# Two cross attentions: head sums in one pass in full precision, and a tail that keeps its tokens on rows

## The chip, the cores and the metric

The kernel runs on one core of a Trainium2 chip. The metric is device time in microseconds of one execution; lower is better. A core has TensorE (PE in the profile, with its weight loads as PEld), VectorE (DVE), ScalarE (ACT), GpSimd (POOL), SyncE (SP), whose only work here is to issue transfers, and 16 DMA engines.

## The reference, cut to what matters

Two decoder layers on x (8 batches of 100 tokens, 256 features), with a context of 8 x 361 rows of 256 features. All data is float32.

```python
x = x + tanh(g_xattn[0]) * xattn0(layernorm(x), ctx)    # 16 heads of 64
x = x + tanh(g_ffn[0])   * ffn0(layernorm(x))           # latent attention, 8 experts + shared one, dense
x = x + tanh(g_xattn[1]) * xattn1(layernorm(x), ctx)    # 16 heads of 16, masked, biases on q, k, v and o
x = x + tanh(g_ffn[1])   * ffn1(layernorm(x))           # 2 of 8 experts for each token, taken by distance
```

xattn0 is not attention over all keys. Each query row i of the 100 meets the keys i, i+100, i+200 and i+300 only (361 keys, the missing ones of the last group are padded), and the softmax runs over these four. ffn1 works like this:

```python
d2 = sum(xs*xs) + sum(centroid*centroid) - 2*xs@centroid.T     # xs is the layer norm of x
dist = sqrt(maximum(d2, 1e-12)); w, sel = top_k(dist, 2); w = softmax(w)
out = sum over the two experts of w * ((silu(xs@Wg+bg) * (xs@W1+b1)) @ W2 + b2)
```

## The kernel before

Features stand on the 128 partitions (two tiles of 128) and the 800 tokens along the free dimension; a `half` is 400 of them. Five engine programs are written out by hand, each a fixed sequence; they meet on semaphores. A product whose operands are split in a rounded high part and a low rest is taken in three one-pass products (fp32r); a product on float32 operands takes four passes and shows as two records of PE.

Stages, with their times in the profiled execution: norm and query of the first cross attention (to 41.5 us), its batch loop (to 223), its output product (to 241), ffn0's attention (to 353), ffn0's experts (to 450), the second cross attention's query and first keys (to about 485), its loop over 32 quads (to 623), its output product, norm and the routing (to 667.8), the 20 blocks of ffn1's experts (to the end).

**First cross attention, batch loop.** For batch b TensorE runs `keys(b)`, eight tiles of six one-pass products each (`project_a`), into PSUM banks 0 and 1, then `values(b-1)`, eight tiles of six products and one that spreads the softmax weights (`SPREAD`, `SES`). VectorE multiplies each key tile by the queries (`products`, L1707) into three `PROD` buffers, and between those runs the seven steps of the previous batch's softmax (L1715 to L1739, on 16 partitions, one for each head). ScalarE rounds each product tile to `PRODH` (L1145), GpSimd takes the rest `PRODL` (L1485), and `sim` sums the features of a head: two one-pass products with 16 output rows for each tile, over all eight tiles into one bank, three tiles behind the keys. Then `weigh` (L1751, L1754) multiplies and sums eight value tiles.

**Second cross attention, quad loop.** Quad q = 4b + g holds four heads of batch b. In iteration q TensorE takes `turned_scores(q)`, the `scores` of quad q+2 whose maxima VectorE finds (`top`, L2049), turns the maxima (L879), and runs `mix_v(q-1)`: 12 products of up to 122 x 32 by 100 columns into bank 6, four of them side by side in groups of 32 output rows. A head gives 16 rows of values and 16 rows of sums (the values buffer holds ones beside each head). When a batch's four quads are in, VectorE's `outs(b)`, in iteration 4b+5, shuffles the sums and copies the mixed rows (L2067, L2069), ScalarE inverts the sums by Ln and Exp, GpSimd divides and adds the value bias into `OT1` (L1565, L1568) and then builds the query slots of a later batch (`mask_queries`). `mix_v(4b+4)` waits for `outs(b)` because it writes the same bank.

**Tail.** Behind the loop TensorE multiplies `OT1` (four groups) by `WO1`: 16 products of 400 columns, half of them behind the last batch's division. ScalarE gates, VectorE adds to X, `norm(5)` follows, normed rows and X are transposed to tokens on rows (`rows_of`: `ROWS`, `RESID`), ScalarE squares them, and 16 small products give the dot products with the centroids. `route()` on VectorE picks two experts for each token, counts, and places each token in blocks of 128. Meanwhile VectorE has split the first expert's weights (`gu_low(0,0)`, `gu_low(0,1)`) right after the loop.

**SP's queue at that place** (order of issue): loads of expert weights 1 and 2, the bias rows, two down tables, a wait for `expert_weights_low_ready` N0+2 (both halves of `gu_low(0,*)`), the load of expert weights 3 into the buffer that these halves have read, a wait for `rows_copied`, the store of `ROWS` to DRAM, the store of `RESID` to the output. GpSimd gathers the first block's rows from DRAM when the first store has landed and `XROW` is known; the first expert product follows.

Of the kernel before, what the change touches and what calls it, by code (L numbers as in the profile page):

```python
# [7 lines left out]
F32 = mybir.dt.float32  # L8
# [15 lines left out]
P = 128  # L24
# [28 lines left out]
def program(nc, t):  # L53

    with ExitStack() as ctx:
# [24 lines left out]
        HS = sb("HS", [P, TI0 * H0])  # L80
# [8 lines left out]
        SM0 = sb("SM0", [H0, 6, S])  # L89
# [12 lines left out]
        def cut(region, at, n, parts=P):  # L102
# [6 lines left out]
        PROD = cut(RW, 8192, 1200).rearrange("p (s c) -> p s c", s=3)  # L109
        VSB = cut(RW, 9392, 1200).rearrange("p (s c) -> p s c", s=3)  # L110
        PV = cut(RW, 10592, 800).rearrange("p (s c) -> p s c", s=2)
        SE = cut(RW, 11392, 1200, H0).rearrange("p (s c) -> p s c", s=3)
# [13 lines left out]
        PRODH = part("PRODH", [P, 4, HALF], "XC", 0)  # L126
        PRODL = part("PRODL", [P, 4, HALF], "Y", 0)
        HSR = part("HSR", [P, TI0 * H0], "RB", 3328 + 4 * HALF)
# [41 lines left out]
        WO1 = cut(RW, 8464, 1024).rearrange("p (g c) -> p g c", g=4)  # L170
# [3 lines left out]

        KTHL = part("KTHL", [P, 2, KD, 2, KVE], "RW", 4032)
# [7 lines left out]
        OT1 = part("OT1", [P, 4, T], "XC", 0, F32)  # L183
        PTC = WK[:, :, :].rearrange("p s c -> p (s c)")[0:CH].rearrange("p (s c q) -> p s c q", s=2, c=3)
        SUMS, UN = STD[:, 0, :], STD[:, 1, :]
# [8 lines left out]
        CSQ = CENTS[0:S, 48:56]  # L194

# [6 lines left out]
        SQUARES = part("SQUARES", [S, B, D], "RO", B * D, F32)  # L202
        POSITION = part("POSITION", [S, 2 * B, P], "RO", B * D)
        RESID = part("RESID", [S, B, D], "RQ", GU1, F32)
# [55 lines left out]
            a_probs_low_ready a_products_high_ready a_products_low_ready a_keys_summed  # L260
# [9 lines left out]
            router_scores_shifted router_function_taken router_high_ready router_weights_spread  # L270
            router_spread_copied router_spread_copied_odd router_squares_ready gate_summed
# [3 lines left out]
            c_pads_set c_keys_summed c_keys_copied c_keys_low_ready c_query_low_ready  # L275
            c_values_summed c_values_copied c_scores_summed c_maximum_found c_maxima_low_ready
            c_maxima_turned c_maxima_placed c_turned_scores_summed c_exp_taken c_heads_mixed
            c_sums_inverted c_mixed_copied c_mixed_biased c_output_summed c_output_gated
            c_added_to_x mask_ready mask_stored c_query_turned_up c_query_stacked_even
            c_query_stacked_odd context_loaded3 c_query_slots_ready c_query_weights_scaled  # L280
# [14 lines left out]
        NORM = [(X, XC, "layer"), (X, Y, "layer"), (Y, XC, 0), (Y, XC, 2), (X, XC, "layer"), (X, XC, "layer")]  # L295
        LAYER = {0: 0, 1: 1, 4: 2, 5: 3}
# [25 lines left out]

        W_PIECES = [9, 11, 13, 15]

        LAG0 = 3

        def key_bank(b, m):

# [159 lines left out]
        def _(pe):  # L488
# [54 lines left out]
            def keys(b):  # L543
                pe.wait_ge(sem["a_context_low_ready"], b + 1)
                for ti in range(TI0):
# [6 lines left out]
                    if ti >= LAG0:  # L552
                        sim(b, ti - LAG0)
# [1834 lines left out]
```

## Time and profile before

| | us |
|---|---|
| median of three runs (lowest, highest) | 837.34 (836.78, 839.22) |
| the profiled execution | 836.42 |
| its span | 834.2 |
| PE busy | 745.0 (89%) |
| DVE busy | 562.8 (67%) |
| ACT busy | 414.6 (50%) |
| POOL busy | 241.5 (29%) |

The span runs from the first instruction to the last; the execution's own time is 2.2 us longer. Busy time is an average over stages with different limits: in the first cross attention VectorE is busy nearly all the time, in the quad loop TensorE works between short waits, and between 623 and 668 us the engines work one after another. PE records overlap each other, so their sum is more than the time the array streams.

### The profile page before, as it was taken

Reading aid. Unit: us, or ns where it says so; the run is one execution under the profiler, and the core shown is the slowest. Engines: PE = TensorE matmul, PEld = TensorE weight load, DVE = VectorE, ACT = ScalarE, POOL = GpSimd, SP = SyncE. Lnnn points to the kernel's source line nnn. Section 1 sums busy time; section 2 is a strip of 40 time slices with the busy share of each in tenths; the row PEclk is TensorE's granted clock in tenths of the full one; section 3 lists DMA queues with packets and bytes.
Section 4 is the critical chain, followed back from the end, with each engine's and each line's share of the span. In section 5 each row is a group of like instructions: output and inputs, shape, how many; then the busy total and the mean of one; then the engine's idle time right before and its main releaser. Section 6 shows DMA issues by size and latency. Waiting matters only on the chain.

```text
span 834.2 us, 13705 instructions
## 1 busy us (share of the span) xinstructions
PE 745.0 (89%) x4761; PEld 621.0 (74%) x4761; DVE 562.8 (67%) x1030; ACT 414.6 (50%) x896; POOL 241.5 (29%) x195
## 2 busy tenths in 40 slices
PE   6999999999889469989998898888998699999996
PEld 3588888889865168657996566666774699999995
DVE  3369999999728979737666567676554666656652
ACT  4544444443253249835434356565664545655651
POOL 0064544444003514510003302222212133433422
PEclk9999999999999979897999899998789599999999
DMA  6400000000070000000000766545052248999972
GB/s 235 200 2 18 19 19 19 19 1 1 1 279 9 0 0 3 1 1 1 1 9 1 182 158 150 132 108 172 2 195 95 86 163 291 328 304 309 328 227 57
DMA packets 29050, 86.01 MB, mean 103 GB/s; under 512 B 3759, under 2 KB 19599, under 8 KB 25655
## 3 DMA queue, kind: packets, MB, share of 16 engines
q1 hardware_dynamic: 25143, 79.89, 29.1%
q0 software_dynamic: 3840, 5.25, 3.0%
q8 instruction: 40, 0.66, 0.3%
q14 instruction: 27, 0.22, 0.1%
HBM read 74.75 MB, written 10.38 MB: 102 GB/s over the span
## 4 chain that ended last, share of the span: by engine, by line
PE 55%; DVE 14%; issue 4%; ACT 3%; DMA 2%; POOL 1%; POOLq 0%; SPq 0%; DVEq 0%; ACTq 0%
PE PS L490 51%; PE PS L1033 1%; DVE SM L2049 1%; DVE WK L1811 1%; DVE RW L1751 1%; PE PS L662 1%; DVE WK L1808 1%; DMA KST<-mask_rows 1%; DVE RO L1754 1%; PE PS L879 1%; PE PS L1003 1%; ACT SQ L1078 1%; POOL OT L1565 0%; DVE M L2058 0%; DMA out<-YO,TROW 0%
## 5 line engine op out<-in xcount | busy, mean ns | idle before, releaser
L1485 POOL TENSOR_TENSOR PRODL<-RW,PRODH 128x361 fp32r<-128x361 f32 x64 | 64.8, 1016 | 114.7 <-ACT PRODH L1145 111.1
L2049 DVE TENSOR_REDUCE SM<-PS 100x1 f32<-100x362 f32 x128 | 64.9, 531 | 46.5 <-PE PS L490 45.7
L490 PE MATMUL PS<-CTXH,WKV0H 128*128 128x362 f32 x256 | 85.8, 335 | 9.5 <-DVE RW L1707 8.9
L490 PE MATMUL PS<-CTXL,WKV0H 128*128 128x362 f32 x256 | 84.1, 328 | 0.0
L490 PE MATMUL PS<-CTXH,WKV0L 128*128 128x362 f32 x256 | 83.9, 328 | 0.0
L1334 ACT ACTIVATE WK<-PS 120x400 f32<-120x400 f32 (+1 forms) x96 | 48.3, 507 | 43.1 <-PE PS L490 42.2
L490 PEld LDWEIGHTS PS<-CTXH,WKV0H 128*128 128x128 f32 x256 | 48.3, 188 | 15.9 <-DVE RW L1707 11.0
L490 PE MATMUL PS<-KST,QST 97*100 97x362 f32 x128 | 54.4, 437 | 5.9 <-DMA KST<-mask_rows 3.3
L1592 POOL DMA_INDIRECT out<-YO,TROW x20 | 31.5, 1573 | 95.2 <-PE PS L1003 45.6
L1145 ACT CAST PRODH<-RW 128x361 fp32r<-128x361 f32 x64 | 31.8, 496 | 53.7 <-DVE RW L1707 53.4
L1754 DVE TENSOR_REDUCE RO<-RW 128x100 f32<-128x400 f32 x64 | 56.1, 877 | 2.2
L490 PE MATMUL PS<-RB,HTT 114*128 114x256 f32 (+1 forms) x240 | 55.2, 379 | 0.6 <-ACT HTT L1433 0.6
L2073 DVE TENSOR_TENSOR GUL<-RB,GUH 128x1368 fp32r<-128x1368 f32 x28 | 44.1, 1579 | 14.3 <-ACT GUH L1372 14.3
L1137 ACT COPY RW<-PS 128x361 f32<-128x361 f32 x64 | 29.5, 462 | 47.8 <-PE PS L490 46.4
L490 PE MATMUL PS<-GUH,XTH 128*128 128x342 f32 x160 | 51.6, 322 | 0.0
L490 PE MATMUL PS<-GUL,XTH 128*128 128x342 f32 x160 | 51.5, 322 | 0.0
L490 PE MATMUL PS<-GUH,XTL 128*128 128x342 f32 x160 | 51.3, 321 | 0.0
L490 PEld LDWEIGHTS PS<-RB,HTT 114*128 114x128 f32 (+1 forms) x240 | 44.7, 189 | 6.2 <-ACT HTT L1433 0.9
L490 PEld LDWEIGHTS PS<-CTXL,WKV0H 128*128 128x128 f32 x256 | 48.6, 190 | 0.0
L490 PEld LDWEIGHTS PS<-CTXH,WKV0L 128*128 128x128 f32 x256 | 48.2, 188 | 0.0
L1565 POOL TENSOR_TENSOR OT<-STD 128x400 f32<-128x400 f32 x8 | 11.2, 1395 | 120.7 <-ACT STD L1349 120.7
L1707 DVE TENSOR_TENSOR RW<-PS,RQ 128x400 f32<-128x400 f32 x64 | 36.2, 567 | 8.4 <-PE PS L490 7.5
(310 smaller groups left out, 1980.8 us busy)
## 6 DMA issues: line engine op xcount, KB each, us to landing
RB<-W SPq DMA_DIRECT2D x14, 1368.0 KB, 6.0
RB<-W SPq DMA_DIRECT2D x20, 768.0 KB, 7.1
KST<-keys_by_head SPq DMA_DIRECT2D x24, 362.0 KB
RQ<-W SPq DMA_DIRECT2D x6, 1368.0 KB, 6.1
keys_by_head<-KTHL SPq DMA_DIRECT2D x8, 724.0 KB, 3.3
CTX<-ctxT SPq DMA_DIRECT2D x16, 361.0 KB, 6.6
RW<-WGU SPq DMA_DIRECT2D x1, 2304.0 KB, 8.5
RW<-WKV SPq DMA_DIRECT2D x1, 2048.0 KB, 9.9
```

The lines of the kernel that those rows point to most:

```text
L490: return pe.matmul(out, lhsT, rhs, start=start, stop=stop)
L662: m = pe.transpose(PS[0:S, 4 + q, x * S:(x + 1) * S], PB[:, i % 3, (4 * q + x) * S:(4 * q + x + 1) * S], IDN[0:S, 0:S])
L1137: act.copy(VSB[:, i % 3, 0:KV], PS[:, 4 + i % 2, 0:KV]).then_inc(sem["a_values_copied"], 1)
L1145: act.copy(PRODH[:, i % 4, 0:KV], PROD[:, i % 3, 0:KV]).then_inc(sem["a_products_high_ready"], 1)
L1334: act.activation(PTC[0:CHT[c], q % 2, c, :], PS[0:CHT[c], 2 + c, 0:4 * S], ACT.Exp).then_inc(sem["c_exp_taken"], 1)
L1485: pool.tensor_tensor(low, raw, high, ALU.subtract).then_inc(sem["a_products_low_ready"], 1)
L1565: pool.tensor_tensor(o, UN.rearrange("p (g c) -> p g c", g=4), SUMS.rearrange("p (g c) -> p g c", g=4), ALU.mult).then_inc(sem["c_mixed_bi ...
L1592: pool.indirect_dma_start(t["out"], bass.IndirectOffsetOnAxis(ap=TROW[:, k:k + 1], axis=0), YO[:, k % 2, :], None, compute_op=ALU.add).the ...
L1707: dve.tensor_tensor(out, k, q, ALU.mult).then_inc(sem["a_products_ready"], 1)
L1754: dve.tensor_reduce(OT0[:, ti, tok(b)], PV[:, i % 2, :].rearrange("p (c i) -> p i c", c=NC), AX_X, ALU.add).then_inc(sem["a_heads_mixed"], 1)
L2049: dve.tensor_reduce(SM1[:, q % 2, j:j + 1], PS[0:S, i % 2, 0:KVE], AX_X, ALU.max, negate=True).then_inc(sem["c_maximum_found"], 1)
L2073: dve.tensor_tensor(GUL[k % 2][:, :, j, :], raw_gu(k, j), GUH[k % 2][:, :, j, :], ALU.subtract).then_inc(sem["expert_weights_low_ready"], 1)
```

## The change

1. First cross attention. `PROD` is kept in float32 in two buffers of four tiles, and `PRODH`, `PRODL` and their work on ScalarE and GpSimd are gone. `sim(b, quad)` takes four tiles at once: four float32 products of 128 x 32 by 361 columns, one to each group of 32 output rows. `sim(b, 0)` stands behind key tile 5, `sim(b, 1)` behind value tile 1 of the batch before. The softmax runs on 128 partitions instead of 16.
2. Second cross attention. `mix_v` reads the values buffer 16 columns earlier for odd quads, so that two quads fill 128 rows; `outs` has two parts of two instructions and a shuffle, each on 200 columns, and `divide` moves to VectorE. The value bias and `WO1` times the centroids are folded once (`fold_output`, `fold_centroids`), dot products of X with the centroids are taken in the loop (`dot_residual`), and X is turned to rows there (`turn_residual`).
3. Output: `project_out(b)` gives tokens on rows for one batch, 8 columns of centroid products and 256 of output in one accumulation of two products of 264 columns. VectorE adds these to the turned X, takes `bn_stats` and `bn_aggr`, and the norm is applied by ScalarE, one instruction for each batch.
4. Order: `gu_low(0,0)` moves into the loop (q = 29), `gu_low(0,1)` behind `route()`.

The diff, cut (semaphore renames and layout lines left out):

```diff
-    for b in range(B): ... (GpSimd: divide, add bias, mask_queries(b + 3))
+    for b in range(3, B):
+        mask_queries(b)
...
     def sim(b, quad):
+        pe.wait_ge(sem["a_products_ready"], 4 * i + 4)
+        for j in range(4):
+            m = mm(PS[32 * j:32 * j + 32, 2 + b % 2, 0:KV], HS[:, 32 * quad:32 * quad + 32],
+                   PROD[i % 2][:, j, 0:KV], quad == 0, quad == 1)
...
+    if (b, g) == (4, 0): fold_output()        # 8 small products, in mix_v
+    if (b, g) == (5, 0): fold_centroids()     # 4
+    if b == 6: dot_residual(g)                # 4 for each g
...
+    def project_out(b):
+        pe.wait_ge(sem["c_mixed_divided"], b + 1)
+        ...
+            pe.wait_ge(sem["c_rows_summed"], b - 2)
+        for c in range(2):
+            m = mm(PS[0:S, (0, 1, 7)[b % 3], 0:8 + D], OT1[:, c, tok(b)], WO1[:, c, :], c == 0, c == 1)
...
+    if q == QUADS: project_out(4)             # ahead of the last mix_v
+    if q in (24, 28, 29, 30): turn_residual(...)
+    if q in (30, 31): project_out(2 * q - 60); project_out(2 * q - 59)
...
     def outs(b):
+        link(dve.tensor_scalar(pair(OPPOSITE), mixed[:, :, 0, :], UPPER, None, ALU.mult))
+        link(dve.scalar_tensor_tensor(pair(OPPOSITE), mixed[:, :, 1, :], LOWER, pair(OPPOSITE), ...))
+        dve.stream_shuffle(SUMS, OPPOSITE, [q ^ 16 for q in range(32)])
+        link(dve.tensor_scalar(pair(UN), mixed[:, :, 0, :], LOWER, None, ALU.mult))
+        dve.scalar_tensor_tensor(pair(UN), mixed[:, :, 1, :], UPPER, pair(UN), ...)
...
+    for b in (5, 6, 7):
+        add_rows_in(b)
+        statistics(b)
     (ScalarE)
+    act.activation(RSTD, MOMENTS[:, :, 1], ACT.Ln, ...); act.activation(RSTD, RSTD, ACT.Exp, scale=-0.5)
+    act.preload_act_table_set("sqrt_and_others")
+    for b in range(B):
+        act.activation(ROWS[:, b, :], RESID[:, b, :], ACT.Identity, bias=SHIFTS[:, b:b + 1],
+                       scale=RSTD[:, b:b + 1]).then_inc(sem["rows_copied"], 1)
...
     route()
+    gu_low(0, 1)
     (SP)
     sp.wait_ge(sem["expert_weights_low_ready"], N0 + 2)
     load_weights(3)
-    sp.wait_ge(sem["rows_copied"], 4)
+    sp.wait_ge(sem["rows_copied"], B)
     sp.dma_start(XROWS..., ROWS)
```

## Rows read from the trace of the kernel before

**Rows 1.** Windows: span, length, busy us of PE, PEld, DVE, ACT, POOL, clock, DMA.
```profile
53.50:206.30 152.80, 144.35 (x851) 132.94 (x851) 145.98 (x224) 66.76 (x133) 73.16 (x64) 1.00 0.05 13
...
482.00:574.40 92.40, 82.79 (x823) 62.90 (x821) 62.89 (x150) 57.78 (x135) 19.60 (x16) 0.98 0.53 133
574.40:623.00 48.60, 42.71 (x463) 34.44 (x463) 26.29 (x70) 31.21 (x70) 8.65 (x8) 0.75 0.33 111
623.00:667.80 44.80, 35.00 (x160) 25.04 (x160) 26.64 (x65) 21.69 (x41) 8.39 (x6) 0.80 0.32 109
```

**Rows 2.** Timeline, first cross attention: start, length, engine, line, names, count, idle before.
```profile
53.51 0.57 DVE L1707 TENSOR_TENSOR RW<-PS,RQ 128x400 f32<-128x400 f32 x1 [3.15 <-PE PS L490]
...
119.83 0.56 DVE L1707 TENSOR_TENSOR RW<-PS,RQ 128x400 f32<-128x400 f32 x1
...
131.12 0.33 PE L490 MATMUL PS<-SES,SPREAD 128*128 128x362 f32 x1
...
132.63 0.33 PE L490 MATMUL PS<-SES,SPREAD 128*128 128x362 f32 x1
...
141.47 0.57 DVE L1707 TENSOR_TENSOR RW<-PS,RQ 128x400 f32<-128x400 f32 x1
```

**Rows 3.** Lines of the softmax: ns minimum/median/maximum, first and last start.
```profile
L1730 DVE TENSOR_TENSOR RW<-RW,SM x8: 561/807/810, 58.9 to 209.8; 16x400 f32<-16x400 f32 x8
...
L1736 DVE CAST SES<-RW x8: 356/653/668, 60.1 to 210.3; 16x400 fp32r<-16x400 f32 x8
...
L1739 DVE TENSOR_TENSOR SES<-RW,SES x8: 565/904/912, 61.3 to 210.7; 16x400 fp32r<-16x400 f32 x8
```

**Rows 4.** Timeline, one mix_v of the quad loop and the load behind it.
```profile
607.24 0.50 PEld L490 LDWEIGHTS PS<-WK,RQ 122*32 122x32 f32 x24 [0.17 <-issue]
...
607.90 0.16 PEld L490 LDWEIGHTS PS<-KST,QST 97*100 97x100 f32 x1 [0.15 <-issue]
```

**Rows 5.** Timeline, outs of one batch.
```profile
543.89 0.60 DVE L2067 STREAM_SHUFFLE STD<-PS 128x400 f32<-128x400 f32 x1
544.38 0.56 DVE L2069 COPY STD<-PS 128x400 f32<-128x400 f32 x1
```

**Rows 6.** Lines by form, quad loop: count, busy us, mean ns, idle before.
```profile
L2012 DVE SCALAR_TENSOR_TENSOR KTHL<-PS,COLS,KTHL 128x361 fp32r<-128x361 f32 x13 | 7.6, 586 | 3.5 <-ACT KTHL L1308 3.5
```

**Rows 7.** Waits of PE from 482 to 623 us: total us, times, longest.
```profile
PE PS L490 <- ACT WK L1334: 6.3, 4, 1.6
PE PS L490 <- DVE STD L2069: 4.8, 3, 1.6
PE PS L879 <- DVE M L2059: 1.6, 4, 0.4
```

**Rows 8.** Timeline, from the last mix_v to the first expert product.
```profile
620.78 2.23 PE L490 MATMUL PS<-WK,RQ 122*32 122x100 f32 x48
...
629.87 5.64 PE L490 MATMUL PS<-OT,RW 128*128 128x400 f32 x16 [0.92 <-POOL OT L1568]
...
646.75 0.32 SPq L470 DMA_DIRECT2D token_rows<-ROWS  x1
...
649.60 0.19 DVE L2124 TENSOR_SCALAR RT<-RT 100x64 f32<-100x64 f32 x1
...
652.80 0.16 DVE L2141 TENSOR_TENSOR RTC<-RT 100x8 f32<-100x8 f32 x1
...
662.12 0.48 DVE L2189 TENSOR_TENSOR WEIGHED<-RB,RT 100x320 fp32r<-100x320 f32 x1
662.39 1.30 POOL L1584 DMA_INDIRECT XB<-token_rows,XROW  x1 [25.29 <-DVE TROW L2186]
...
667.81 0.62 PE L490 MATMUL PS<-BROWS,PICKB 128*128 128x342 f32 x1 [1.02 <-issue]
```

**Rows 9.** Window of the small centroid products: PE records, clock.
```profile
645.30:646.90 1.60, 1.60 (x21) 1.00 0.00 0
```

**Rows 10.** Transfers from 621 to 660 us: count, KB each, us from issue to landing.
```profile
RB<-W SPq DMA_DIRECT2D x1, 1368.0 KB, 5.7
```

More of the change, by code:

```diff
@@ L439, in _ @@
             load(CENT, t["centT"], "moe1_small_loaded")
+            sp.wait_ge(sem["norm_variance_summed"], 10)
+            load(WO1T, t["WO1T"], "moe1_small_loaded")
             for b in range(B - 3):
@@ L589, in _ @@
                 else:
-                    for ti in range(TI0 - LAG0, TI0):
-                        sim(0, ti)
+                    sim(0, 1)
             project_out_a(0, 0)
@@ L911, in _ @@
                 ahead = q + 2 < QUADS
+                if q == QUADS:
+                    project_out(4)
                 if 0 <= q < QUADS:
@@ new lines, in outs @@
+                if b == 6:
+                    dve.tensor_copy(DOTS, PS[0:S, 6, 400:464].rearrange("p (b e) -> p b e", b=B))
+                dve.scalar_tensor_tensor(pair(UN), mixed[:, :, 1, :], UPPER, pair(UN), ALU.mult,
+                                         ALU.add).then_inc(sem["c_mixed_copied"], 1)
+                if b == 4:
+                    dve.tensor_tensor(CENT2, CENT2, ASIDE[:, 0:8].unsqueeze(1).to_broadcast([P, KD, 8]),
+                                      ALU.subtract).then_inc(sem["router_operand_ready"], 1)
@@ L2071, in gu_low, with statistics @@
+            def statistics(b):
+                dve.wait_ge(sem["c_rows_summed"], b + 1)
+                link(dve.bn_stats(PARTS6[:, b, :], RESID[:, b, :]))
+                dve.bn_aggr(MOMENTS[:, b, :], PARTS6[:, b, :]).then_inc(sem["c_statistics_found"], 1)
             def gu_low(k, j):
@@ L2081, in _ @@
                     top(q + 2, 1)
+                if g == 0 and b >= 2:
+                    divide(b - 2)
                 if g == 1 and b >= 1:
                     outs(b - 1)
+                if q == 29:
+                    dve.wait_ge(sem["c_values_summed"], 2 * B)
+                    gu_low(0, 0)
                 if g in (1, 2) and 0 <= b and b + 3 < B:
@@ L2091, in _ @@
                     keys_lo(2, q + 2)
-                if q == 24:
-                    dve.wait_ge(sem["moe1_small_loaded"], 32)
+                if q == 26:
+                    dve.wait_ge(sem["moe1_small_loaded"], 48)
                     dve.tensor_copy(PICKB[:, 0:E1], PICKED).then_inc(sem["router_result_ready"], 1)
+                    dve.wait_ge(sem["c_turned_scores_summed"], 12 * 6)
+                    dve.tensor_copy(TRI[:, :], TRIANGLE)
                 if q == -2:
                     stack_odd(1)
-            outs(B - 1)
-            dve.wait_ge(sem["router_scores_summed"], 2)
-            link(dve.tensor_copy(CSQ, PS[0:S, 7, 0:8]))
-            dve.tensor_copy(TRI[:, :], TRIANGLE)
-            gu_low(0, 0)
-            gu_low(0, 1)
-            add_to_x("c_output_gated", "c_added_to_x")
-            norm(5)
-            for i in range(4):
-                dve.wait_ge(sem["moe_turned"], 2 + i + 1)
-                dve.tensor_copy(ROWS[:, 2 * i:2 * i + 2, :],
-                                PS[0:S, i, :].rearrange("p (x c) -> p x c", x=2)).then_inc(sem["rows_copied"], 1)
+            for b in (0, 1):
+                add_rows_in(b)
+            for b in (0, 1):
+                statistics(b)
+            divide(B - 2)
+            for b in (2, 3):
+                add_rows_in(b)
+                statistics(b)
+            outs(B - 1)
+            add_rows_in(4)
+            statistics(4)
+            divide(B - 1)
+            for b in (5, 6, 7):
+                add_rows_in(b)
+                statistics(b)
             def route():
```

399 lines of the change are left out of this document (212 added, 187 removed).

## The prediction

> **What bounds the kernel now.** I read the windows by stage first [rows 1]. In the first cross attention's batch loop VectorE is busy 146.0 of 152.8 us at full clock: it sets the pace, TensorE is close behind. In the quad loop TensorE is busy about 88%, up to 574 us at clock 0.98, after that at 0.75, and the last twelve quads take 48.6 us. From 623.0, where the last mix_v ends (620.78 + 2.23), to the first expert product at 667.81 the engines work in turn [rows 8]: 44.8 us, which the change is meant to shorten. The timeline and the waits then give what each part waits for.
>
> **First cross attention.** A batch takes 141.47 - 119.83 = 21.64 us [rows 2]. Three softmax lines run in 0.81, 0.65 and 0.90 us while GpSimd splits products, and in 0.56, 0.36 and 0.57 at the last batch, where it doesn't [rows 3]. With that work gone each batch is 0.25 + 0.29 shorter, and the third line, now a scalar_tensor_tensor of 0.63 (0.586 for 361 elements [rows 6], plus 39 at 1.04 ns), 0.27: 0.8 on VectorE. 128 partitions instead of 16 cost nothing in the same number of elements a partition. ScalarE and GpSimd lose work that stood beside VectorE's; worth nothing itself.
>
> On TensorE nine one-pass products lie between two spreads, 132.63 - 131.12 = 1.51, so 0.167 each [rows 2]. A batch's 16 head sums cost 2.67. Eight float32 products of 400 columns end at 5.64 less the last record's own 0.3 or so, 5.33: 0.167 a pass [rows 8], so 361 columns in four passes are 0.60. Four side by side: mix_v's 12 products of 100 columns load and stream in about 0.5 [rows 4], where one after another they would be 12 x 0.167 = 2.0. So a quad is 0.60 where groups overlap (2.41 where not), and mix_v has a gap of 0.17 before and 0.15 behind [rows 4]; I count 0.16 once, as the other lies under the product in flight: 0.76.
>
> The Trainium skill, "TensorEngine Tiling (Array Packing)", Key Properties, says that changing the tiling mode drains TensorE, which speaks against a head sum of two quads for each batch among full-width products. By that rule both gaps are exposed and a quad is 0.92, with 0.3 us more for each batch and 2 in all; the gaps of [rows 4] allow either.
>
> From the batch's first product to the second spread is 131.12 - 119.83 = 11.29 [rows 2], with 14 of the 16 head sums (2.34); two quads are 1.52, and the first waits about 0.4 longer for key tile 5. So the second weighing starts 0.4 earlier, and the sum pair that stands ahead of the third is gone: 0.57 for each batch, seven times, 4.0. In batch 0, VectorE waits 3.15 before 53.51 [rows 2], behind sums that go through ScalarE and GpSimd; I take half of it, 1.6. Together -5.6. Bounds: -1.6 (TensorE gives nothing back) and -1.6 - 7 x 0.8 = -7.2.
>
> **Quad loop.** outs took 544.94 - 543.89 = 1.05 [rows 5] and mix_v(4b+4) waits for it: of PE's waits, seven of up to 1.6, 11.1 in all, stand at that place (ScalarE's exponential ends at the same moment) [rows 7]. New: four instructions of 200 elements, 0.586 - 161 x 1.04 ns = 0.42 each [rows 6], a shuffle of 0.60 - 0.21 = 0.39 [rows 5], three links of 0.04: 2.1. That is 1.05 more, seven times, 7.35, all exposed, as the next instruction of PE is that mix_v. Four waits on L2059 (1.6 in all [rows 7]) fall where GpSimd builds slots beside the maxima's split; these slots now start as soon as a batch is scored: -1.6. divide (0.37) and the smaller Ln and Exp lie beside TensorE.
>
> Moved into PE's queue ahead of the last mix_v: 28 small products (8, 4 and 16). 21 records, 10.5 products, take 1.60 [rows 9]: 0.15 each, 4.2. Small copies inside three outs, 0.8. Four turns of four transposes, 128 columns in four passes, 0.21 each, 3.4. Five project_out of two products of 264 columns, 0.44 each, 4.4. Sum with the above: 7.35 - 1.6 + 4.2 + 0.8 + 3.4 + 4.4 = 18.6. gu_low(0,0) at q = 29 delays the last maxima by 1.6, under a turn and the turned scores; with it about 1.0 of the added work lies in existing waits. 17.6.
>
> The Trainium skill, "TensorEngine Tiling (Array Packing)", Instruction Overhead, gives a product about 60 cycles however few its columns. At 2.4 GHz and four passes that is an estimate of 0.10 for a small product, 2.8 instead of 4.2 for the 28; the row shows 0.15, and I go by the row.
>
> The clock: after 574 the stretch has 0.75, so half of it runs at 1.2 GHz [rows 1]. The products alone would need 0.75 x 48.6 = 36.5 at full clock; with the waits as they are I take 40. More work without gaps may keep the clock up; I take a gain of 4 of the 8.6, bounds +4 (the slow share also covers the added work) and -8.6. So the last mix_v ends 17.6 - 4 = 13.6 later (9.0 to 21.6).
>
> **Tail.** Let M be the end of the last mix_v (623.0 before). Removed: 16 products of 400 columns (10.7), the norm, both row turns, the squares. New on VectorE: outs(7) 2.1, add_rows of 264 elements 0.43 (rate as above) and statistics (256 elements 0.42, a small one 0.2, links 0.05) for batches 4 to 7, four times 1.15, divide 0.37: M+7.2. ScalarE's Ln and Exp of 8 elements 0.5, six short VectorE instructions 1.3: L2124 at M+9.1, where it was 649.60 - 623.0 = M+26.6 [rows 8]. bn_stats has no row: 0.2 to 0.9 for 256 elements moves this by -0.9 to +1.9.
>
> Then 3.2 to L2141 (652.80 - 649.60), which waits for ScalarE's square root. That one now stands behind a table load (1.3), eight ROWS instructions (about 0.33 each), the bias rows (1.3) and gu_high(1,0) (1.3): M+14.4 instead of M+12.3, a stall of 2.1. From L2141 to the end of L2189 9.8 (662.60 - 652.80 [rows 8]): M+24.4 with the clock as it is.
>
> Now SP. Its queue waits for both halves of gu_low(0,*) before weights 3 and the store of ROWS. gu_low(0,1) now stands behind route(): +1.6, M+26.0. The weights land 5.7 later [rows 10], the store's 800 KB lie behind them, about 4.6 more: M+36.3. Before, the store went at 646.75 and was down long before the gather at 662.39 [rows 8]. From gather to first expert product 667.81 - 662.39 = 5.4: M+41.7 instead of M+44.8. So 3.1 is saved of the 16 that were in reach; the row store is late next. Bounds: -6 (weights and rows go side by side) to +1.
>
> ffn1's blocks keep their work. Sum: -5.6 + 13.6 - 3.1 = +4.9, so 836.42 + 4.9 = 841.3 for the profiled execution; the median is 0.9 above that execution: **842.2**.
>
> **Rivals.**
> (1) Faster: the loop hides what is added. PE waits 12.7 in these rows [rows 7]; were the small products and turns to fill that time and the clock to stay up, M would be 2 later, not 13.6: 830.6. For it: these waits are as long as the work. Against: outs lengthens the wait itself, and folds and dots stand behind it in PE's queue. It decides when M moves by less than 5. Chance 0.15.
> (2) The clock alone: full throughout, M 9.0 later: 837.6, no change. A clock of 0.75 with TensorE busy at 88% says that it hangs on little [rows 1]. 0.19.
> (3) Slower still: the added work runs at half clock: M +21.6: 850.2. 0.15.
> (4) The four groups don't overlap: a quad 2.57 instead of 0.76, 3.6 a batch, 29 in all: 871. [rows 4] speak against it. 0.03.
> (5) My forecast, 837.5 to 848: 0.48.
>
> **How the numbers follow.** 0.3% (2.5 us), about what a measurement tells from no change, puts the borders at 834.8 and 839.9. Faster: rival 1 and a fifth of rival 2, 0.19. Same: the rest of rival 2 and the low end of the forecast, 0.22. Slower: 0.59. Range 832 to 852: it leaves out rival 1 below 832 (0.10), rival 4 (0.03) and the upper end of rival 3 (0.05).
>
> **What would show it.** Head-sum quads at 0.75 to 0.95 and a batch at 21.0 to 21.2; L1730 at 0.56; mix_v after outs waiting 2.6 instead of 1.6; the last mix_v 9 to 18 later relative to the loop's start; L2124 9 behind it; the store of rows issued behind L2073 and the gather waiting for it, not for XROW. I am wrong if the store lands before XROW is known, or if the loop grows by less than 5.

## The result and the profile after

The changed kernel takes 860.76 us (median of 4 runs, 859.82 to 861.42), the kernel before beside it 837.53 (836.78 to 839.22): ratio 1.0285, 95% interval 1.0264 to 1.0307, slower. Forecast were 842.2 and 832 to 852, so it came out slower as expected, and by far more. The profiled execution of the changed kernel has a span of 858.9 us, against 834.2: 24.7 more.

The head of its page (instructions; busy time and share; the granted clock in 40 slices):

```profile
span 858.9 us, 13415 instructions
PE 738.6 (86%) x4749; PEld 614.0 (71%) x4749; DVE 564.8 (66%) x1077; ACT 375.8 (44%) x816; POOL 163.7 (19%) x119
PEclk9999999999999699889999998878787589999999
```

TensorE does no more than before and the program is longer; the row of the clock has sevens and a five in its last third. The windows by stage of the kernel after, columns as in [rows 1] (window, length, busy us of PE, PEld, DVE, ACT, POOL, clock, DMA share and GB/s): quad loop from the first to the last mix_v, from there to the first expert product, and the rest.

```profile
490.95:649.39 158.44, 137.64 (x1334) 110.11 (x1333) 94.33 (x253) 83.31 (x197) 21.00 (x14) 0.84 0.43 113
649.39:692.09 42.70, 12.65 (x57) 10.68 (x56) 21.85 (x70) 13.62 (x21) 2.38 (x3) 0.56 0.28 96
692.09:858.90 166.81, 159.14 (x958) 150.38 (x958) 94.53 (x124) 85.15 (x135) 55.28 (x38) 0.98 0.77 251
```

The loop and the experts of the kernel before, cut at the same instructions (its tail stands in [rows 1]):

```profile
491.52:623.00 131.48, 116.86 (x1242) 91.24 (x1241) 83.56 (x206) 83.62 (x193) 28.25 (x24) 0.90 0.48 129
...
667.81:834.20 166.39, 159.08 (x958) 150.34 (x958) 94.53 (x124) 85.07 (x135) 57.11 (x38) 0.98 0.76 251
```

That places all of it. The loop's first mix_v is 0.6 earlier, the loop 27.0 longer, the tail 2.1 shorter, the experts 0.4 longer: 24.7. The experts' blocks are what they were; the tail is as forecast; the loop is not.

**Inside the loop.** TensorE's waits there (us in all, times, longest), to be held against [rows 7]:

```profile
PE PS L494 <- DVE STD L2094: 13.3, 5, 2.8
PE PS L494 <- DVE CENTS L2097: 3.1, 1, 3.1
PE PS L494 <- issue: 2.7, 1, 2.7
PE PS L884 <- DVE M L2071: 0.6, 2, 0.4
```

The seven waits behind outs are now 2.6 to 3.1 and make 19.1 (the first three rows; the wait put down to `issue` stands at the same place, in batch 4). That is the 2.6 forecast, and the four waits of the maxima's split, 1.6 before, are 0.6. One of them on the timeline (start, length, engine, line, names, count, idle before), and the clock around it by windows:

```profile
525.62 0.34 PE L884 MATMUL PS<-IDN,M 100*32 100x100 f32 x2
528.55 1.23 PE L494 MATMUL PS<-WK,RQ 122*32 122x100 f32 x24 [2.59 <-DVE STD L2094]
...
534.94 0.73 PE L494 MATMUL PS<-WK,RQ 122*32 122x100 f32 x24
```

```profile
528.00:534.80 6.80, 6.25 (x40) 4.78 (x40) 3.09 (x8) 1.34 (x3) 0.00 (x0) 0.50 0.01 2
534.80:548.40 13.60, 11.52 (x126) 8.92 (x124) 9.55 (x26) 9.48 (x24) 3.00 (x2) 1.00 0.69 166
```

At the end of the wait the clock is at its lower level, 1.2 GHz, for 6.8 us; the mix_v in it takes 1.23, the one behind it 0.73. The same happens at 510.9 (3.4 us), 548.5 (6.8), 568.9 (10.2), 592.8 (10.2) and 613.3 (13.7): 51.2 us of the loop (its clock of 0.84 says the same: (1 - 0.84) x 2 x 158.44 = 50.7), each stretch beginning at a wait for outs or within 1.6 us behind one. Before it was 27.3, at 527.5, 578.7, 595.7 and 616.2.

**Tail.** From the last mix_v on, to be held against [rows 8]:

```profile
648.66 0.73 PE L494 MATMUL PS<-WK,RQ 122*32 122x100 f32 x24
...
657.75 0.20 DVE L2185 TENSOR_SCALAR RT<-RT 100x64 f32<-100x64 f32 x1
...
664.42 0.17 DVE L2202 TENSOR_TENSOR RTC<-RT 100x8 f32<-100x8 f32 x1 [3.38 <-ACT RT L1478]
...
676.37 0.33 SPq L357 DMA_DIRECT2D RB<-W  x1
676.74 0.37 SPq L474 DMA_DIRECT2D token_rows<-ROWS  x1
...
686.94 1.21 POOL L1607 DMA_INDIRECT XB<-token_rows,XROW  x1 [37.26 <-DMA token_rows<-ROWS]
690.38 0.69 PE L1043 MATMUL PS<-IDN,XB 128*128 128x128 f32 x2 [11.87 <-DMA XB<-token_rows,XROW]
...
692.09 0.62 PE L494 MATMUL PS<-BROWS,PICKB 128*128 128x342 f32 x1 [1.02 <-issue]
```

With M = 649.4: distances at M+8.4 (forecast 9.1), L2202 at M+15.0 (14.4), route's end at M+25.4 (24.4), the rows stored from M+27.3, down at M+37.5 (36.3), first expert product M+42.7 (41.7). The gather waits for the store, named in its own row, as forecast.

**First cross attention.** One batch of the kernel after: a key tile, the first quad of head sums and the next tile; the second quad and the second spread; and the batch's first and the next batch's first product (for [rows 2]).

```profile
119.55 0.57 DVE L1719 TENSOR_TENSOR PROD<-PS,RQ 128x400 f32<-128x400 f32 x1
...
123.86 0.43 PE L494 MATMUL PS<-CTXH,WKV0H 128*128 128x362 f32 x1 [0.32 <-DVE PROD L1719]
...
124.80 0.33 PE L494 MATMUL PS<-CTXH,WKV0L 128*128 128x362 f32 x1
125.05 0.81 PE L494 MATMUL PS<-PROD,HS 128*32 128x361 f32 x8
125.80 0.43 PE L494 MATMUL PS<-CTXH,WKV0H 128*128 128x362 f32 x1
126.07 0.33 PE L494 MATMUL PS<-CTXL,WKV0H 128*128 128x362 f32 x1
...
130.14 0.81 PE L494 MATMUL PS<-PROD,HS 128*32 128x361 f32 x8
130.89 0.43 PE L494 MATMUL PS<-SES,SPREAD 128*128 128x362 f32 x1
...
141.23 0.57 DVE L1719 TENSOR_TENSOR PROD<-PS,RQ 128x400 f32<-128x400 f32 x1
```

The batch takes 21.68 (before 21.64). The eight records of a quad lie in 0.81: the four row groups do overlap. But from the product at 124.80 to the one at 126.07 it is 1.27, where one-pass products 0.167 apart would need 0.33: a quad costs 0.93, the 0.60 of its columns and both gaps of about 0.16. The Trainium skill, "TensorEngine Tiling (Array Packing)", Key Properties, says that a change of the tiling mode drains TensorE; the prediction's sum by that rule was 0.92 a quad, and the trace agrees with it, not with the 0.76 that I took.

The softmax lines (ns minimum/median/maximum), for [rows 3], and what GpSimd did beside the slow ones:

```profile
L1742 DVE TENSOR_TENSOR RW<-RW,SM x8: 565/566/2545, 57.5 to 209.8; 128x400 f32<-128x400 f32 x8
L1748 DVE CAST SES<-RW x8: 352/359/1576, 59.7 to 210.4; 128x400 fp32r<-128x400 f32 x8
L1751 DVE SCALAR_TENSOR_TENSOR SES<-SES,HS,RW x8: 620/626/635, 60.5 to 210.8; 128x400 fp32r<-128x400 f32 x8
```

```profile
79.48 2.38 POOL L1516 TENSOR_TENSOR WOUT0L<-RW,WOUT0H 128x1024 fp32r<-128x1024 f32 x1 [20.60 <-ACT WOUT0H L1194]
79.75 2.54 DVE L1742 TENSOR_TENSOR RW<-RW,SM 128x400 f32<-128x400 f32 x1
```

The medians are the 0.56, 0.36 and 0.63 of the forecast. The maxima stand in batches 1 and 2 and are new: GpSimd, with the product splits gone, comes to the splits of the output weights 7.5 us earlier in its queue (before at 86.95, in the weighing), and there they meet a VectorE instruction with two operands in SBUF: 1.78 and 2.54 instead of 0.57. The Trainium skill, "GPSIMD Engine Reference", Specifications, lists the SBUF interfaces as shared with VectorE where it has two SBUF inputs; this row agrees.

### The profile page after: what moved, and what is told of

Read it like the earlier page. It is cut to its first block, busy times and chain, and to the rows that moved or that the text cites. A ratio compares the mean times of both kernels' runs of the same rounds, so it can differ in the third digit from the quotient of the medians.

```text
span 858.9 us, 13415 instructions
## 1 busy us (share of the span) xinstructions
PE 738.6 (86%) x4749; PEld 614.0 (71%) x4749; DVE 564.8 (66%) x1077; ACT 375.8 (44%) x816; POOL 163.7 (19%) x119
## 4 chain that ended last, share of the span: by engine, by line
PE 62%; DVE 20%; issue 8%; DMA 4%; ACT 4%; SPq 1%; POOLq 0%; DVEq 0%; ACTq 0%
PE PS L494 58%; DVE RW L1763 3%; DVE SM L2061 2%; DVE RO L1766 1%; PE PS L1073 1%; DVE WK L1823 1%; SPq L357 1%; PE PS L665 1%; DMA token_rows<-ROWS 1%; DVE WK L1820 1%; DVE PROD L1719 1%; DMA KST<-mask_rows 1%; DVE SM L1736 1%; PE PS L884 1%; DMA RW<-WQ 1%
## 5 line engine op out<-in xcount | busy, mean ns | idle before, releaser
L494 PE MATMUL PS<-CTXH,WKV0H 128*128 128x362 f32 x256 | 87.7, 343 | 14.0 <-DVE PROD L1719 13.4
L494 PE MATMUL PS<-KST,QST 97*100 97x362 f32 x128 | 57.5, 461 | 5.0 <-DMA KST<-mask_rows 3.2
L1719 DVE TENSOR_TENSOR PROD<-PS,RQ 128x400 f32<-128x400 f32 x64 | 36.4, 570 | 10.6 <-PE PS L494 9.8
L1580 POOL TENSOR_TENSOR QST<-QALL,COLS 96x800 fp32r<-96x800 f32 x15 | 22.9, 1546 | 105.3 <-PE PS L494 95.8
L2278 DVE TENSOR_TENSOR STD<-PS,SIL 128x342 f32<-128x342 f32 x40 | 20.4, 511 | 31.7 <-PE PS L494 31.7
L494 PEld LDWEIGHTS PS<-QST,KST 101*120 101x120 f32 (+1 forms) x192 | 38.4, 212 | 4.0 <-issue 2.1
```

What stands on the lines that cost most here:

```text
L494: return pe.matmul(out, lhsT, rhs, start=start, stop=stop)
L1580: pool.tensor_tensor(QST[b % 3][0:96, :, u, :], QALL[0:96, :, tok(b)].bitcast(F32), COLS[0:96, 21 + u:22 + u].unsqueeze(2).to_broadcast([9 ...
L1719: dve.tensor_tensor(out, k, q, ALU.mult).then_inc(sem["a_products_ready"], 1)
L2278: dve.tensor_tensor(H1T[:, j, :], PS[:, 2 * j + 1, 0:HH], SIL1[:, j, :], ALU.mult).then_inc(sem["hidden_ready"], 1)
```

## Experiments

Theory after the traces: the loop is longer by about 10 us of added work, 6 of waiting and 10 to 11 that come from the clock, which falls where TensorE waits longer. Rivals: a wait costs only its length; the small products, not the waits, lower the clock; the tail or the head sums are to blame. Each run has the kernel before beside it on the same chip; that one's median was 835.4 to 836.7 in these calls, single executions 832.4 to 841, and single ones of some variants spread as far. Ratios are to it, with the 95% interval. A filler is a product whose result nobody reads.

| run | edit | us | ratio |
|---|---|---|---|
| e1 | before + head sums | 835.5 | 1.000 (0.998 to 1.002) |
| e2 | before + 1.2 us in seven waits | 853.4 | 1.022 (1.019 to 1.025) |
| e3 | after, waits filled | 841.9 | 1.008 (1.005 to 1.011) |
| e4 | after, bank copied first | 855.5 | 1.023 (1.019 to 1.027) |
| e5 | after, rows stored first | 852.4 | 1.019 (1.016 to 1.022) |
| e6 | before, waits filled | 831.1 | 0.995 (0.992 to 0.997) |
| e7 | after without small products | 849.2 | 1.019 (1.013 to 1.024) |
| e8 | e3 + e5 + square root + tail filled | 833.5 | 0.997 (0.994 to 0.999) |
| e9 | before + small products | 850.1 | 1.017 (1.015 to 1.020) |
| e10 | e5, gu_low(0,1) early | 846.9 | 1.015 (1.012 to 1.017) |
| e11 | e8, gu_low(0,1) early | 829.2 | 0.993 (0.991 to 0.996) |
| e12 | e11 + e4, one filler each | 839.3 | 1.005 (1.002 to 1.008) |
| e13 | after, folds two quads later | 858.1 | 1.027 (1.022 to 1.032) |
| e14 | e1, output weights later | 836.1 | 1.000 (0.998 to 1.002) |
| e15 | e14, product ahead of the sum | 832.0 | 0.995 (0.993 to 0.997) |
| e16 | e11 + e13 + e14 + e15 | 828.9 | 0.991 (0.988 to 0.995) |

**e1, the head sums alone.** All edits of the first cross attention on the kernel before.

> The kernel before with the first cross attention's half of the change alone (head sums in full precision in four row groups, no splits into high and low). Theory, from the trace after: batch 0 gets 1.45 us shorter and the other batches nothing, since a quad of sums costs TensorE 0.93 instead of 0.76 and stands ahead of the second spread, and the first two batches lose some of it again where GpSimd splits the output weights: -0.6 us in all, 836.9. Rival, the prediction's sum: -5.6, 831.9. Second rival: the change of the loop's start shifts the clock's episodes, and the time moves by more than 2 us either way with no batch changed.

835.5 against 835.6: no gain, and 5.6 us would lie well outside the interval. The time from batch 1's first product to the first of batch 7 is 132.6, as in the changed kernel (132.5; before 131.1); batch 0 is 1.43 shorter. The prediction's -5.6 is wrong; -0.6 can't be told from nothing here.

**e2, the waits alone.** In outs of the kernel before, batches 0 to 6:

```diff
+                    link(dve.stream_shuffle(SUMS, PS[:, 6, 0:4 * S], [16 + q % 16 for q in range(32)]))
+                    link(dve.tensor_copy(UN, PS[:, 6, 0:4 * S]))
                 dve.stream_shuffle(SUMS, PS[:, 6, 0:4 * S],
```

> The kernel before, unchanged but for two more VectorE instructions (a second shuffle and a second copy of the same 400 columns, some 1.1 us with their links) in outs of batches 0 to 6, so that TensorE waits 2.65 us instead of 1.6 at seven places. Nothing is added to TensorE. Clock theory: the longer waits let the clock fall at more of these seven places, so on top of 7.7 us of waiting there are 6 to 11 us at half clock: 851 to 857. Rival: a wait costs its own length only, and the clock in the trace after fell for the added small products: 845.

+17.8 us for seven waits of 2.83 instead of 1.58, 8.8 of waiting. TensorE's waits and the loop's window:

```profile
PE PS L490 <- DVE STD L2072: 19.9, 7, 2.9
```

```profile
491.44:638.78 147.34, 123.51 (x1242) 94.75 (x1241) 92.34 (x227) 83.66 (x193) 28.25 (x24) 0.85 0.44 115
```

The same 1242 records take TensorE 123.5 us instead of 116.9 and the clock is 0.85 instead of 0.90. It now falls at every one of the seven waits. The loop is 15.9 longer, the tail 1.0. So 8.8 us of waiting brought 6.6 more in the loop through the clock, and 17.8 in all; the rival that a wait costs its length only (845) is out.

**e3 and e6, the waits filled.** Ahead of the wait for outs, in the changed kernel (five products) and in the one before (two), result not used:

```diff
             def mix_v(q):
                 b, g = divmod(q, 4)
+                if g == 0 and b:
+                    pe.wait_ge(sem["c_maxima_placed"], 2 * q + 6)
+                    for i in range(5):
+                        mm(PS[:, 5, 200:400], AVG[:, :], CS[:, :, :].rearrange("p k c -> p (k c)"), True, True)
                 pe.wait_ge(sem["c_exp_taken"], 3 * q + 3)
```

> The kernel after, with five products of 200 columns (1.7 us together at full clock) into unused columns ahead of each of the seven waits for outs, result not used. The waits end when they did. Clock theory: TensorE no longer stands still there, the clock stays up more, and 5 to 11 of the 25.7 us at half clock's cost come back: 850 to 856. Rival (the waits are not what lowers the clock): 861 or up to 2 us more, as some of the filler stands behind the wait's end.

> The kernel before with two products of 200 columns (0.67 us together) into unused columns ahead of each of the seven waits for outs, result not used, so that TensorE stands still 0.9 and 0.1 instead of 1.58 us there. Clock theory: most of the 12.6 us that half clock costs in the quad loop goes: 825 to 832. Rival (before's clock fell for another reason than these waits): 836 to 838.

The window of the loop and the filler's own group (records; busy us, mean ns; idle before), of e3 and then of e6:

```profile
487.42:629.01 141.59, 132.08 (x1404) 105.65 (x1403) 94.08 (x253) 83.28 (x197) 20.98 (x14) 0.99 0.47 126
```

```profile
L494 PE MATMUL PS<-CS,AVG 128*128 128x200 f32 x70 | 13.7, 343 | 6.7 <-ACT QST L1373 6.7
```

```profile
491.34:616.78 125.44, 112.66 (x1270) 86.78 (x1269) 84.58 (x206) 83.65 (x193) 28.14 (x24) 1.00 0.51 136
```

```profile
L490 PE MATMUL PS<-CS,AVG 128*128 128x200 f32 x28 | 6.6, 359 | 6.4 <-ACT QST L1346 6.4
```

Giving TensorE 13.7 us of useless work makes the changed kernel faster by 18.9 us (860.8 to 841.9; 17.0 by the ratios), more than either side had said, and 6.6 us of it the kernel before 5.6 faster. The loops are 16.9 and 6.0 shorter; in e3's trace 3.5 more were saved ahead of the loop, where nothing was edited. TensorE goes on no earlier (0.98 us of wait and 1.96 of filler stand where 2.59 of wait stood); only the clock is different, 0.99 and 1.00. These two windows also give the work at full clock: 132.1 - 13.7 - 1.7 (half of its 3.4 us at the lower level) = 116.7 after, 112.7 - 6.6 = 106.1 before. So of the loop's 27.0, 10.6 is added work, 10.1 is clock (137.6 - 116.7 = 20.9 against 116.9 - 106.1 = 10.8), and 6.2 is TensorE idle (20.8 against 14.6). A second estimate of the clock's part takes half of TensorE's busy time within the stretches at the lower level, 48.4 us after and 25.9 before: 24.2 - 12.9 = 11.3, which leaves 9.5 for the work.

**e4, a shorter wait.** outs in two steps: one copy of the bank, which lets TensorE go on, then masks and shuffle from the copy behind the batch's maxima.

```diff
+                dve.tensor_copy(RAWMIX, PS[:, 6, 0:4 * S]).then_inc(sem["c_bank_copied"], 1)
...
-                        pe.wait_ge(sem["c_mixed_copied"], 2 * b)
+                        pe.wait_ge(sem["c_bank_copied"], b)
```

> The kernel after, with outs in two steps for batches 0 to 6: one copy of the 400 columns out of the bank (0.56 us), which lets TensorE go on, and the masks, the shuffle and the second half from that copy behind the batch's maxima. TensorE's wait is about 1.5 us shorter at seven places. Waits alone: -10.5, 850. Clock theory: another 5 to 11 us, 839 to 845. Rival: VectorE's later maxima give the time back, as it now has 0.5 more to do for each batch: 855 to 861.

855.5, the rival's case. The wait for outs is 1.08 to 1.55, but TensorE now also waits for the maxima, which VectorE reaches later:

```profile
PE PS L494 <- DVE SQ L2089: 5.8, 5, 1.3
PE PS L494 <- DVE SM L2061: 4.7, 5, 1.2
```

The clock of the loop is 0.89 (0.84) and still falls at five places, where no single wait is longer than 1.6.

**e5 and e10, the row store.** The store of ROWS ahead of the wait and the load of expert 3's weights; e10 has gu_low(0,1) in VectorE's wait for the square root as well.

```diff
-            sp.wait_ge(sem["expert_weights_low_ready"], N0 + 2)
-            load_weights(3)
             sp.wait_ge(sem["rows_copied"], B)
             sp.dma_start(XROWS.rearrange("(b s) c -> s b c", s=S), ROWS[:, :, :]).then_inc(sem["rows_stored"], 16)
+            sp.wait_ge(sem["expert_weights_low_ready"], N0 + 2)
+            load_weights(3)
```

> The kernel after with SP's queue changed at one place: the store of ROWS stands ahead of the wait for gu_low(0,*) and of the weights of expert 3, so it is issued when ScalarE has the rows (about 12 us behind the last mix_v, M) and not at M+27.3. The prediction's account of the tail (row store late next): the gather starts once XROW is known, M+24.5, and the first expert product comes at M+30 instead of M+42.7, 12 earlier: 848 to 850. Rival: the weights of expert 3 are late next or the store shares its engines with the other loads: 853 to 861.

> e5 with gu_low(0,1) moved into VectorE's wait for the square root (3.4 us long, so it costs nothing there). SP then issues the weights of expert 3 at about M+14 instead of M+27.3, and they are down before the gather. If it is that load which made the gather take 9.1 us instead of 3.4: 5.6 less than e5, 845 to 848. Rival (the gather is slower since it follows XROW with no distance, or for another reason): 852 as e5.

Of e5 and then of e10, the load, the gather and the first turn of its tokens (the stores were issued at 661.4 and 657.8):

```profile
674.21 2.77 POOL L1607 DMA_INDIRECT XB<-token_rows,XROW  x1 [24.97 <-DVE TROW L2247]
675.93 0.33 SPq L357 DMA_DIRECT2D RB<-W  x1
683.28 0.69 PE L1043 MATMUL PS<-IDN,XB 128*128 128x128 f32 x2 [5.21 <-DMA XB<-token_rows,XROW]
```

```profile
658.52 0.33 SPq L357 DMA_DIRECT2D RB<-W  x1
670.60 1.29 POOL L1607 DMA_INDIRECT XB<-token_rows,XROW  x1 [24.96 <-DVE TROW L2248]
674.31 0.69 PE L1043 MATMUL PS<-IDN,XB 128*128 128x128 f32 x2
```

In e5 the gather waits for the routing, as it should, but the tokens come 9.1 us later instead of 3.4: the 1.4 MB of weights are issued 1.7 behind it, and both are in flight at once. M to first product is 36.0 (42.7). With the load out of the way the tokens take 3.7 and it is 30.7. So the store held the tail as forecast, and behind it stood a collision that the forecast did not see. The whole times are 852.4, between the two ranges expected, and 846.9; the distances from M are the better measure, as e10's loop, the same program as e5's, was 4.3 us shorter in its trace (154.1 against 158.4).

**e7, e9 and e13, the small products.** e7 leaves fold_output, fold_centroids and dot_residual out of the changed kernel, so that its router chooses by other numbers; e9 puts as many products of 8 columns into the kernel before; e13 moves the two folds:

```diff
-                if (b, g) == (4, 0):
+                if (b, g) == (4, 2):
                     fold_output()
-                if (b, g) == (5, 0):
+                if (b, g) == (5, 2):
                     fold_centroids()
```

> The kernel after without the products of fold_output, fold_centroids and dot_residual (32 centroid products and the folded bias, 44 products in all): these values are left out, so the router chooses by other numbers. Theory: work of 0.1 to 0.15 each at full clock, 4 to 6 us, and where they run at half clock once more 3: 851 to 855; the clock still falls at the waits, and most of its cost stays. Rival: it is the small products that lower the clock, by keeping TensorE's array empty: without them 838 to 846.

> The kernel before with 28 products of 8 columns in the places of the changed kernel's (8, 4 and 16, each batch of them behind a wait for outs and ahead of the mix_v), result not used; outs and its wait of 1.58 stay as they are. If a small product costs its 0.15 to 0.2 and no more: +5, 841. Clock theory widened by e7 (small products right behind a wait lengthen the stretch in which TensorE does little): the clock falls more often in batches 4 to 6, where it falls before already, and stays low longer: 843 to 848.

> The kernel after with the 12 small products of fold_output and fold_centroids ahead of mix_v(18) and mix_v(22) instead of mix_v(16) and mix_v(20), so that they no longer stand right behind a wait of 2.6 us. Same work. If what lowers the clock is a stretch in which a wait and small products come together: two of the seven low stretches get shorter and the products run at full clock, 2.5 to 6 us less, 855 to 858. If each lowers it by itself: 860 to 862.

(They are 28 products, 56 records, not the 44 of the expectation.) e7: 11.6 us less by the medians, 8.4 by the ratios, its four executions from 847.5 to 855.2; e9: 14.7 more, beyond both sides. Their own busy time in e9 and the loop's windows of e7 and e9:

```profile
L490 PE MATMUL PS<-CS,AVG 128*128 128x8 f32 x56 | 8.1, 274 | 4.8 <-DVE STD L2071 3.2 <-ACT WK L1336 1.6
```

```profile
491.97:635.39 143.42, 123.18 (x1278) 95.76 (x1277) 94.58 (x253) 83.26 (x197) 20.98 (x14) 0.90 0.47 125
```

```profile
492.56:633.23 140.67, 125.00 (x1298) 98.88 (x1297) 84.31 (x206) 83.72 (x193) 28.25 (x24) 0.89 0.45 120
```

So the small products cost 8.1 and not 4.2, partly because they run at the lower clock; in e3, nearly all at full clock, they were 6.2. In e9 that is also all that they cost TensorE in the loop: its busy time grows by 8.1 (116.9 to 125.0), so the other products are as fast as before. The loop is 9.2 longer; 4.7 more stand in stages where the two kernels have the same instructions (1.0 ahead of the loop, 2.1 in the tail, 1.6 in the experts), and these runs don't explain them.

e7's loop is 15.0 shorter, but not all of that belongs to the small products. From the first mix_v to the end of the wait in batch 4 the changed kernel and e7 run the same instructions, none of them small; the first row is the changed kernel's, the second e7's:

```profile
490.95:569.57 78.62, 67.57 (x658) 51.92 (x657) 51.17 (x134) 44.35 (x108) 11.99 (x8) 0.89 0.57 133
```

```profile
491.97:566.26 74.29, 63.12 (x657) 47.88 (x657) 50.95 (x134) 44.27 (x108) 11.98 (x8) 0.98 0.60 141
```

4.3 of the 15.0 are there: the same program came at a clock of 0.89 and of 0.98. In e10 this stretch takes 75.97, in e13 79.86. The loop in all traces (in e4 and e12, whose waits are others, the lower level lasts 34.1 and 30.7):

| trace | wait for outs | small products | us at the lower level in the loop |
|---|---|---|---|
| before; e1, e14, e15 | 1.6 | no | 27.3; 23.8, 25.9, 30.6 |
| e9 | 1.6 | yes | 29.8 |
| e7 | 2.7 | no | 27.3 |
| after; e5, e10, e13 | 2.7 | yes | 51.2; 51.2, 37.5, 54.6 |
| e2 | 2.8 | no | 43.3 |
| e6 | filled | no | 0.0 |
| e3, e8, e11, e16 | filled | yes | 3.4, 0.0, 6.8, 3.4 |

That the waits are needed for the fall is shown by the last two rows, and that longer ones can lengthen it by e2. That the small products lower the clock isn't shown: e9 against before says that they don't, e7 against after that they do beside longer waits, with one trace of e7 and a spread as large as in e5 and e10. e13's 858.1 (ratio 1.027) can't be told from the change's 1.0285, and its loop has 0.83: that they stand right behind a wait is not what counts, at least for these 12.

**e8, e11, e12, the tail and the waits together.** e8 is e3 and e5 with ScalarE's square root ahead of the bias rows and of gu_high(1,0), and filler ahead of TensorE's three waits in route; e11 moves gu_low(0,1); e12 adds e4 with one filler product a wait.

```diff
+            fill(12)
             pe.wait_ge(sem["router_result_ready"], 4)
...
+                gu_low(0, 1)
                 dve.wait_ge(sem["router_function_taken"], 2)
```

> The kernel after with the waits filled as in e3, the rows stored first as in e5, ScalarE's square root ahead of the bias rows and of gu_high(1,0), and in the tail 12, 12 and 2 products of 200 columns (0.33 each at full clock), result not used, ahead of TensorE's three waits for route. e3 measured 841.9; the store gives 12, the square root's order 2.4, the clock in the tail 3 to 4 (its 41 products of 3.5 and 3.6 us halved) : 822 to 827. Rival: the filler in the tail runs at half clock itself and stands in front of the router's products: 828 to 835.

> e8 with gu_low(0,1) in VectorE's wait for the square root, which is 0.9 us there, so 0.7 is paid. If the load of expert 3's weights is what the gather met: 833.5 - 5.6 + 0.7 = 828.6. Otherwise 834.

> e11 with outs in two steps as in e4 and one product of filler for each wait instead of five. The loop without half clock: waits 1.1 instead of 2.6 at seven places and VectorE's maxima later; e3's loop took 141.6 us with 11.7 us of filler in waits. 7 x 1.2 = 8 less than e11, of which later maxima give back some 3 to 5: 824 to 827. If one product is too little to keep the clock up: 830 to 838.

e8, 833.5, missed 822 to 827 by the collision of e5 (its tokens take 8.9); the number lies in the rival's range, but for another reason; e11 is 829.2, 4.3 less than e8. Its gather starts 2.6 earlier behind M than e10's: the earlier square root accounts for 1.8 of that (its wait is 0.9 and not 3.4, and 0.7 of gu_low(0,1) is paid), and 0.6 for a shorter wait for TensorE's products of the slots (0.77 instead of 1.41), which the filler may have given. But the tokens then take 4.5 and not 3.7, so that M to the first product is 28.8, only 1.9 less. e12 fell back to 839.3, slower than either side had said, with a clock of 0.90 in the loop: one filler product in a wait and e4's later maxima are not enough to keep it up. What a wait may be before the clock falls, these runs don't settle.

**e14, e15, e16, the first cross attention.** e14 makes GpSimd's output-weight splits wait for the softmax; e15 also lets VectorE's third key product and those behind it go one place ahead of the softmax's sum.

```diff
                     pool.wait_ge(sem["a_output_weights_high_ready"], b)
+                    pool.wait_ge(sem["a_probs_low_ready"], b)
...
                     products(b, [ti])
-                    if b and ti < 7:
-                        softmax_a(b - 1, ti)
+                    if b and ti != 2:
+                        softmax_a(b - 1, ti - (ti > 2))
```

> e1 (the first cross attention's half alone) with GpSimd's two splits of the output weights waiting for the softmax of their batch, as they came behind it in the kernel before, where the queue's own order did that. L1742 took 1.78 and 2.54 us beside them instead of 0.56 and L1748 once 1.58 instead of 0.36; so 0.5 us in batch 1 and 1.9 in batch 2 come back, less what the splits cost beside the weighing (before: 0.7 each): 1.0 to 2.4 less in the first cross attention, batches 1 and 2 at 21.7 to 22.4 us. Rival: they slow the weighing by as much, nothing changes. The whole time, 835.5 +- 3 in either case, says little; the batch starts in the trace decide.

> e14 with VectorE's third to eighth key product of a batch one place further ahead, in front of the softmax's sum over the keys (0.91 us, with a wait for ScalarE's exponential ahead of it), which holds up key tile 5 on TensorE by 0.47 us. Theory of why the prediction's 0.57 a batch did not come: the quads cost 0.93 each and TensorE waits 0.47 here, so its chain sets the second spread; without this wait a batch takes 0.3 to 0.5 less, 21.2 to 21.4. Rival: VectorE's own row of instructions sets the period (all of them together are 21.0): 21.6 stays.

> e11 (829.2) with e13, e14 and e15 in it: folds two quads later 0 to -2, the first cross attention -3 to -5: 823 to 828. Rival: the filled waits have already taken what e13 gives, and e14 and e15 give nothing: 829.

In e14 batches 1 and 2 take 23.00 and 22.96, together no less than e1's 22.2 and 23.6: the split met the next VectorE instruction with two operands in SBUF, CTXL, 2.89 instead of 0.90.

```profile
82.53 2.39 POOL L1467 TENSOR_TENSOR WOUT0L<-RW,WOUT0H 128x1024 fp32r<-128x1024 f32 x1 [20.57 <-DVE SES L1703]
82.79 2.89 DVE L1651 TENSOR_TENSOR CTXL<-CTX,CTXH 128x722 fp32r<-128x722 f32 x1
```

In e15 they take 21.6 each, and the others 21.56 (115.94 to 137.50), only 0.12 less: the wait of key tile 5 was not what held the batch. The 4 us that e15 is faster than e14 are mostly the 2.8 of batches 1 and 2: in the new order CTXL is done when the split starts, and no instruction is held. e16, 828.9, has everything and takes 0.991 (0.988 to 0.995) of the kernel before; it can't be told from e11, though its trace has the shorter batches of e15.

## Why the prediction was right and wrong

- **Head sums, -5.6: wrong, -0.6.** The terms on VectorE came (three lines at 0.56, 0.36, 0.63; batch 0 1.43 of 1.6). The step that failed here, 5.0 of the 19.8 us between forecast and trace, is the one behind them, "the second weighing starts 0.4 earlier, and the sum pair that stands ahead of the third is gone: 0.57 for each batch". A quad is 0.93 and not 0.76, which takes 0.34 a batch, so the second spread comes 11.34 behind the batch's first product (11.29 before). The third weighing comes at 13.36, at 132.91 (13.21): with the second at its old place, VectorE's own pairs of 1.4 to 1.55 follow, and the pair gone from TensorE's queue was hidden behind them. The 0.57 itself doesn't follow from its text either: 0.4 and a pair of 0.33 would be 0.73. In batch 2 the earlier output-weight split costs what batch 0 gained.
- **outs, +7.35: right.** The waits are 2.6 or a little more, four instructions and the shuffle take 2.1 (649.46 to 651.54 for the last batch). Idle time in the loop grew by 6.2; the prediction's waits sum to 7.35 - 1.6 + 0.8 - 1.0 = 5.6. (Its own terms add to 2.19 and not 2.1, 0.6 in seven waits.)
- **Added work, 12.0: about right, 10.6.** By e3's rows small products 6.2 instead of 4.2 (0.2 each, and not the 0.15 of [rows 9]), turns 2.4 instead of 3.4, output products 5.3 instead of 4.4. These rows overlap their neighbours, so they add to more than the 10.6.
- **The clock, "More work without gaps may keep the clock up; I take a gain of 4 of the 8.6, bounds +4": this is the step that failed, and it is most of the forecast's error.** The clock cost 10 to 11 more instead of 4 less. Both halves of the step were wrong. The work did not come without gaps: the same text had the wait of each batch at 2.6 instead of 1.6. And the bound of +4 let only the added work run slow, while e2 shows a longer wait slowing work that was there before. From -4 to +10.1 is 14.1; the loop missed by 13.4 (27.0 against 13.6), as the other terms were 0.8 too high together. How large the cost is changes from one execution to another: in e10's trace of the same loop half of the busy time at the lower level is 17.9, 5.0 more than before and not 11.3. What lengthened the slow stretches from 27.3 to 51.2, the longer waits alone or together with the added work, stays open; that they vanish when the waits are filled is shown.
- **Tail, -3.1: right, -2.1**, through every station within 1.3, with the row store late as named. That its removal would be met by the weights' load stood in one of the bounds only ("weights and rows go side by side").
- **Rivals.** The third, added work at half clock, was the nearest in kind, and its 850.2 too low, since it counted added work alone. The second asked for a full clock and 837.6; with the waits filled, e3, it is 841.9, and the head sums account for the rest. The first is out: the loop grew by 27.0. Of the signs named, the quads, L1730, the waits, L2124 and the gather's wait for the store came; the batch of 21.0 to 21.2 and the 9 to 18 of the last mix_v did not.

## What to carry to other kernels

Where a stretch shows a clock below 1, every edit in it can have a second price: count TensorE's waits, one for each place, and take their growth once and twice as the two ends (e7's trace shows once, e2 twice); then ask for the same stretch with the waits filled, which is one run and gives work and clock apart. Look at more than one trace, as the same instructions came at 0.89 and at 0.98. A wait that can't be shortened can be filled with products whose result nobody reads; that was worth about 17 us here. One short filler in a wait was not enough (e12). An engine that a change frees comes to its next instructions earlier: look up in its queue what those are, and what on the other engines they will then run beside.

## What had not been expected of the hardware

Seven waits longer by 1.25 us each made a kernel that otherwise did the same 17.8 us slower. The same stretch of the same instructions took 74.3, 76.0, 78.6 and 79.9 us in four traces, by its clock alone. Products of 8 columns, 28 of them, were busy for 6.2 us at full clock and 8.1 in e9, 0.2 to 0.3 each. GpSimd's split of 1024 columns beside a VectorE instruction with two SBUF operands held that one for 2.54 instead of 0.57 and 2.89 instead of 0.90, about its own length; a cast from SBUF to SBUF beside another split of GpSimd's took 1.58 instead of 0.36; the products, with one operand in PSUM, kept their 0.57. A gather of 128 rows took 9.1 instead of 3.4 to 3.7 us with a 1.4 MB load issued 1.7 us behind it.
